# Second attention's projection moved from a block of its own into the first experts' stage

## The reference

```
x = LN(x + softmax attention with RoPE(x))        # layer 0
x = LN(x + sum over 8 experts of w_e * down_e(glu(gate_e x, up_e x)))   # top 2 of 8
x = LN(x + Wo . taylor attention(Wq x, Wk x, Wv x))   # layer 1, 16 heads of 16 features
x = LN(x + capacity-limited experts(x))
```

## Time and profile before

| | us |
|---|---|
| median of 3 runs (850.43 to 851.65) | 851.11 |
| the profiled execution, its own time | 849.08 |
| its span, first to last instruction | 847.0 |
| TensorE busy | 663.2 (78%) |
| VectorE busy | 549.6 (65%) |
| ScalarE busy | 439.5 (52%) |
| GpSimd busy | 406.1 (48%) |

### The profile page before, as it was taken

The page is one execution under the profiler, slowest core; times in us unless marked ns, Lnnn a source line. Parts: engine busy times, 40 slices in busy tenths (PEclk is TensorE's granted clock), DMA queues, the critical chain, the costliest instruction groups (busy, mean ns, idle before and its releaser), DMA issues. The chain is left out here.

```text
span 847.0 us, 18177 instructions
## 1 busy us (share of the span) xinstructions
PE 663.2 (78%) x6567; PEld 417.2 (49%) x6567; DVE 549.6 (65%) x1574; ACT 439.5 (52%) x658; POOL 406.1 (48%) x583
## 2 busy tenths in 40 slices
PE   7748999999869999999977759999996414987500
PEld 3423555555535666666653436767674203555400
DVE  5967888888558898888897653454456883222126
ACT  5433777777745555555526656676763540332102
POOL 7854777777740000000016765666664503788743
PEclk9975999999989999999999988999998755999765
DMA  4773463432000000000004889777851070355354
GB/s 158 240 228 97 122 182 98 119 87 70 4 1 1 1 1 2 1 1 1 2 0 156 253 269 215 190 187 189 198 140 48 11 205 24 79 119 100 32 98 121
DMA packets 134982, 85.79 MB, mean 101 GB/s; under 512 B 11248, under 2 KB 131568, under 8 KB 134768
## 3 DMA queue, kind: packets, MB, share of 16 engines
q1 hardware_dynamic: 128112, 79.33, 34.2%
q0 software_dynamic: 5632, 4.33, 3.7%
q10 hardware_dynamic: 1152, 0.98, 0.4%
HBM read 54.73 MB, written 29.49 MB: 99 GB/s over the span
## 5 line engine op out<-in xcount | busy, mean ns | idle before, releaser
L2143 ACT ACTIVATE a_prob<-a_ps_pair 128x1024 f32<-128x1024 f32 x96 | 93.2, 1024 | 48.1 <-PE a_ps_pair L1979 36.4
L1814 ACT ACTIVATE a_prob<-a_ps_pair 128x1024 f32<-128x1024 f32 x96 | 96.5, 1024 | 13.5 <-PE a_ps_pair L1617 10.7
L2155 POOL TENSOR_SCALAR_AFFINE_SELECT a_prob<-a_prob 128x512 f32<-128x512 f32 (+1 forms) x96 | 76.6, 806 | 51.1 <-ACT a_prob L2143 50.9
L1855 POOL TENSOR_SCALAR_AFFINE_SELECT a_prob<-a_prob 128x512 f32<-128x512 f32 (+1 forms) x96 | 75.6, 789 | 41.2 <-ACT a_prob L1814 40.6
L1753 DVE TENSOR_REDUCE a_mx<-a_ps_pair 128x4 f32<-128x1024 f32 x64 | 77.7, 1220 | 24.3 <-PE a_ps_pair L1658 22.5
L922 POOL TENSOR_SCALAR xn<-xn,stats,norm_b_rstd 128x128 f32<-128x128 f32 x8 | 6.4, 806 | 175.0 <-POOLq L411 175.0
L478 PEld LDWEIGHTS m_ps_n<-wd,m_act 128*128 128x128 f32 x512 | 66.3, 192 | 29.1 <-issue 27.4
L701 ACT ACTIVATE m_up<-m_ps_u,m_bup 128x512 f32<-128x512 f32 x64 | 44.0, 688 | 65.5 <-PE m_ps_u L466 65.5
L590 DVE SCALAR_TENSOR_TENSOR xn<-m_ps_n,m_wt,xn 128x128 f32<-128x128 f32 x256 | 71.7, 342 | 0.2 <-DVE xn L590 0.2
L478 PE MATMUL m_ps_n<-wd,m_act 128*128 128x128 f32 x512 | 67.5, 275 | 1.0 <-DVE xn L590 0.8
L466 PE MATMUL m_ps_u<-m_x1T,wgu 128*128 128x512 f32 x128 | 67.2, 607 | 0.0
(11 more groups left out here) (289 smaller groups left out, 1530.6 us busy)
## 6 DMA issues: line engine op xcount, KB each, us to landing
qst<-scratch_q SPq DMA_DIRECT2D x64, 128.0 KB, 3.0
kst<-scratch_k SPq DMA_DIRECT2D x64, 128.0 KB, 3.1
scratch_q<-p_parts SPq DMA_DIRECT2D x16, 384.0 KB, 2.4
scratch_k<-p_parts SPq DMA_DIRECT2D x16, 384.0 KB, 2.7
qst<-scratch_q SPq DMA_DIRECT2D x32, 192.0 KB, 2.9
kst<-scratch_k SPq DMA_DIRECT2D x32, 192.0 KB, 3.4
c_w<-in_w SPq DMA_DIRECT2D x8, 578.0 KB, 4.0
scratch_q<-parts SPq DMA_DIRECT2D x16, 256.0 KB, 2.5
```

The costliest lines, as they stand in the source:

```text
L1814: nc.scalar.activation(prob[:, r % 6, :], pair[(0, 2, 1)[j]][:, :], ACT.Exp, scale=scale, bias=0.0).then_inc(s_e, 1)
L1855: nc.gpsimd.affine_select(out=blk, in_=blk, compare_op=ALU.is_ge, fill=0.0, base=0, pattern=[[0, n], [1, P]], channel_multiplier=-1).then_ ...
L2143: nc.scalar.activation(prob[:, r % 6, :], pair[r % 2][:, :], ACT.Square, scale=scale, bias=1.0).then_inc(s_e, 1)
L2155: nc.gpsimd.affine_select(out=blk, in_=blk, compare_op=ALU.is_ge, fill=0.0, base=0, pattern=[[0, n], [1, P]], channel_multiplier=-1).then_ ...
```

## The change

The projection of layer 1 becomes steps in `expert_layer0`, and the block `project_layer1` goes. A chunk's rows are normalised as soon as its experts are done: VectorE takes the statistics and a seed of the root, GpSimd refines it in three Newton turns (14 small instructions, each waiting for the one before), ScalarE normalises two tiles and GpSimd two. Five units after that, in six consecutive units, TensorE's turn ends with one step each: the four transposes, four projections, and v. All of these use one PSUM bank, `ps_d`, so each projection waits until the residual of the one before has been taken. VectorE takes a residual first in its turn. The last chunk (`tail`) has no units behind it; it comes after the loop and uses the four banks of gate and up. The bias of all chunks now uses `ps_r`, and its units are moved by one or two. Scratch is laid out by sequence, a store is two DMAs, and four slots are loaded ahead.

```diff
-BUFS1, AHEAD1 = 4, 2
+BUFS1, AHEAD1 = 4, 4
-        turn_at = [E - 1] + [E * c + 2 for c in range(1, NCH)]
-        bias_at = [E + 1] + [E * c + 4 for c in range(1, NCH)]
+        turn_at = [E - 2] + [E * c + 3 for c in range(1, NCH)]
+        bias_at = [E - 1] + [E * c + 5 for c in range(1, NCH)]
+        stats_at = [E * c + E + 1 for c in range(NCH - 1)]
+        next_at = [E * c + E + 5 for c in range(NCH - 1)]
+        next_steps = {n0 + i: (c, i) for c, n0 in enumerate(next_at) for i in range(6)}
 # SyncE
+                    for b in range(2):
+                        sp.dma_start(scratch[i // 2][2 * c + b, :, half:half + P, :].rearrange("s p t -> p s t"),
+                                     parts[:, n % PBUFS, :, T * b:T * b + T]).then_inc(s_store[n % PBUFS], 16)
+                    if 7 <= n < 7 + AHEAD1:
...
+                        load_slot(sp, n - 7, stacks, scratch, s_first)
 # TensorE
+                def turn_next(c):
+                    pe.wait_ge(s_x2a, 2 * c + 2)
+                    pe.wait_ge(s_x2p, 2 * c + 2)
...
+                def project(n):
+                    c, i = n // 4, n % 4
+                    pe.wait_ge(s_xT2, c + 1)
+                    if c < tail:
+                        after(pe, s_r1, n if i else 0)
+                    nc.tensor.matmul(projected(n)[:, :], wqk[:, i, :], x2T[:, c % 2, :], start=True, stop=True).then_inc(s_proj, 1)
...
                 for n in (units - 2, units - 1):
                     reduce(n)
+                for n in range(units, max(next_steps) + 1):
+                    next_layer(*next_steps[n])
+                turn_next(tail)
+                for i in range(4):
+                    project(4 * tail + i)
+                project_v(tail)
 # VectorE
                 for n in range(3, units):
+                    if n - 1 in next_steps and 1 <= next_steps[n - 1][1] < 5:
+                        residual(4 * next_steps[n - 1][0] + next_steps[n - 1][1] - 1)
                     clip(n)
...
+                    if n in stats_at:
+                        row_stats(stats_at.index(n))
+                    if n - 1 in stats_at:
+                        seed_root(stats_at.index(n - 1))
                 for n in (units - 2, units - 1):
                     accumulate(n)
-                row_stats(NCH - 1)
-                merge_rows(NCH - 1)
+                row_stats(tail)
+                seed_root(tail)
+                for n in range(units - 1, max(next_steps) + 1):
+                    if 1 <= next_steps[n][1] < 5:
+                        residual(4 * next_steps[n][0] + next_steps[n][1] - 1)
+                for i in range(4):
+                    residual(4 * tail + i)
 # ScalarE, after take_gate(n)
+                    if n in next_at:
+                        renormalise(next_at.index(n))
+                    if n in next_steps:
+                        next_layer(*next_steps[n])
 # GpSimd
                 for c in range(NCH):
+                    refine_root(c)
                     for i in range(4):
...
+                        lo(4 * c + i)
```

More of the change, by code:

```diff
@@ L369, in expert_layer0 @@
         bns = sb("bns", [P, NTILE, 6])
+        wqk, wv1 = consts["later"]["wqk1"], consts["later"]["wv1"]
+        var2, root, rstd2, shift2 = [sb(n, [P, NTILE]) for n in ("var2", "root", "rstd2", "shift2")]
+        x2T = sb("x2T", [P, 2, CH])
+        resid = sb("resid", [P, 2, CH])
+        parts = sb("parts", [P, PBUFS, NPART, CH], BF16)
         ps_g = [ps(f"ps_g{i}", [P, CH]) for i in range(2)]
@@ L407, in expert_layer0 @@
+        s_lo = sem("lo_done")
+        s_store = [sem(f"parts_stored{i}") for i in range(PBUFS)]
+        s_first = sem("first_stacks_loaded")
+        s_vp = sem("v_projected")
+        s_vc = sem("v_copied")
+        s_ones = sem("ones_set")
         groups = ((0, 2), (2, NCH))
         units = E * NCH
[L409 to L411 removed]
+        turn_at = [E - 2] + [E * c + 3 for c in range(1, NCH)]
@@ L457, in add_bias @@
                         here = slice(t * P, (t + 1) * P)
-                        last = nc.tensor.matmul(ps_bias[c % 2][:, here], wT[:, c % 2, here], bd[:, :], start=True, stop=True)
+                        last = nc.tensor.matmul(ps_r[:, here], wT[:, c % 2, here], bd[:, :], start=True, stop=True)
                     last.then_inc(s_bm, 1)
@@ L739, in _ @@
                         copy_weights(turn_at.index(n))
+                    if n in next_at:
+                        renormalise(next_at.index(n))
+                    if n in next_steps:
+                        next_layer(*next_steps[n])
+                for n in range(units, max(next_steps) + 1):
+                    next_layer(*next_steps[n])
+                renormalise(tail)
+                copy_x2(tail)
+                hi(4 * tail)
+                for n in range(4 * tail + 1, 4 * tail + 4):
+                    hi(n)
+                    mid(n - 1)
+                copy_v(tail)
+                mid(4 * tail + 3)
             @block.gpsimd
@@ L750, in _ @@
                         nc.gpsimd.memset(wT[:, :, :], 0.0).then_inc(s_wTz, 1)
[L752 to L790, removed]
-        x2T = sb("x2T", [P, 2, CH])
-        resid = sb("resid", [P, 4, CH])
-        parts = sb("parts", [P, 8, 3, CH], BF16)
-        ps_qk = [ps(f"ps_qk{i}", [P, CH]) for i in range(4)]
-        ps_x = [ps(f"ps_x{i}", [P, CH]) for i in range(2)]
-        ps_v = ps("ps_v", [P, CH])
-        s_ones = sem("ones_set")
-        s_inv = sem("spread_inverted")
-        s_x2 = sem("tile_normalised")
-        s_x2p = sem("tile_normalised_by_pool")
-        s_xp = sem("x_transposed")
-        s_xT = sem("x_rows_copied")
-        s_proj = sem("qk_projected")
-        s_hi = sem("hi_done")
-        s_r1 = sem("residual_done")
-        s_mid = sem("mid_done")
-        s_lo = sem("lo_done")
-        s_store = [sem(f"parts_stored{i}") for i in range(8)]
-        s_first = sem("first_stacks_loaded")
-        s_vp = sem("v_projected")
-        s_vc = sem("v_copied")
-        def part(c, i, level):
-            return parts[:, 4 * (c % 2) + i, PART_ORDER[i // 2][level], :]
-        with nc.Block() as block:
-            @block.sync
-            def _(sp):
@@ L941, in invert_seed, with load_slot @@
+def load_slot(sp, u, stacks, scratch, done):
+    h0 = UH * (u % 2)
+    for st, sc, runs in zip(stacks, scratch, (SLOT_RUNS["q"], SLOT_RUNS["k"])):
+        src = sc[u // 2, :, :, :].rearrange("s (d h) t -> (s d) h t", h=H)[:, h0:h0 + UH, :]
+        for s0, part, n in runs:
+            sp.dma_start(st[FD * s0:FD * (s0 + n), u % BUFS1, :, :], src[FD * part:FD * (part + n), :, :]).then_inc(done, 16)
 def invert_seed(nc, ve, sem, var, x, t, out):
```

268 lines of the change are left out of this document (139 added, 129 removed).

## The result

The changed kernel takes 855.26 us (median of 5 runs, 853.52 to 855.97) where the kernel before took 850.43 beside it (848.81 to 851.65): ratio 1.0057, 95% interval 1.0041 to 1.0072, 4.8 us slower. The forecast was 852.3, 1.2 us slower.

A forecast was written before the change was run, and what follows sets the result against it. TensorE was taken to fill the expert stage, while no engine fills the projection block. 35.6 us added before unit 63 less 34.4 saved behind it gave 1.2 slower, 852.3 us; own range 850 to 855, 8 in 10 845.5 to 859.5.

The forecast's parts named there:

- Inserted work, 30.0: Before unit 63: TensorE's added transposes, projections and v matmuls, 4.78 us a chunk, paid one for one, together 30.0 us.
- Waits of 0.35 a chunk: Expert units: TensorE waits about 0.2 us for v's bank and 0.15 for renormalised tiles, 2.1 for six chunks.
- Chunk 0, 3.5: Chunk 0's transposes wait for a late root and tiles: 3.9 us, of which 3.5 counted after clearing VectorE's backlog.
- I take 0.28: GpSimd's 14 root steps priced at 0.28 us each, from a 16-element chain, so 3.9 us a refinement.
- TensorE would have come to these transposes at 295.6: Chunk 0: when TensorE would reach the transposes, against tiles ready at 299.5, which gave the 3.9 us wait.
- Cover of 1.7 us in the later chunks: Later chunks: root and tiles done at 14.6 us, TensorE at the transposes at 16.3, leaving 1.7 spare.
- Tail 40.2: From unit 63's start to the next stage: a serial chain at 1.2 GHz, 40.2 us, 34.4 less than before.
- rival 1: Tail runs at the fast clock level: about 4 to 5 us less, 848; chance 0.28.
- The stage behind, nothing: Next stage: two more slots loaded ahead and rows lying together were taken to save nothing.
- rival 4: Loads did hold back the next stage's start and the new layout frees it: 4 us less, 848; chance 0.04.
- Rival 2: GpSimd and VectorE exclude each other, making GpSimd late to every chunk: 5 to 9 us more, 859; chance 0.22.
- Rival 3: TensorE's clock falls in chunk 0's wait of some 2.5 us: slow spells cost 3 us, 855; chance 0.06.

The follow-up runs named there:

- the last kernel: Chunk 0's early seed with reordered, filled tail, plus from chunk 1 on statistics one unit later and root on VectorE, and tail residual earlier: 837.62 us, ratio 0.9859.
- The early seed in chunk 0: Against the changed kernel, only chunk 0's root seed runs in the unit of its row statistics, not one unit later: 851.38 us, ratio 1.0020.

## Why the prediction was right or wrong

Slower was the likeliest side, and the kernel is slower; most of the mechanism held, while one path was half wrong and several terms were mis-sized. 855.26 lies just past the forecast's own range (850 to 855) and inside the range for 8 times in 10. The forecast of 1.2 us was the difference of two sums of about 35, smaller than the miss of a single term below, so its side owes something to luck. By the prediction's own terms:

- *Inserted work, 30.0.* Right: units 3.47 apart, and the doubled projections and the last kernel's chunk of 26.97 show it one for one.
- *Waits of 0.35 a chunk.* 27.45 - 22.21 - 4.78 = 0.46, 0.7 us more over six chunks. It is all v's wait, 0.48 and not 0.2; the transposes' 0.15 isn't seen in the steady chunk.
- *Chunk 0, 3.5.* This is the step that failed by most. From unit 13 to 21 it is 33.33 us, 5.88 over a steady chunk; before, the same stretch was 22.71, 0.50 over. So 5.4, 1.9 more than forecast. The seed came when it was forecast, 48.6 us after the stage's first instruction (293.9 - 245.26 there, 296.31 - 247.67 here). What failed is "I take 0.28": the 14 steps took 5.56, 0.40 each, beside VectorE, and the two tiles 1.82 for 1.7; together 1.8 more, which is the miss. A second step failed without showing in the sum: "TensorE would have come to these transposes at 295.6", 50.3 us after the stage's first instruction. It came 54.2 us after it (303.86 - 1.97 = 301.89), because it had waited 2.24 for VectorE and then ran at the low clock. With steps of 0.28 the tiles would have been ready at about that moment (303.76 - 1.8), so that 3.5 would have come out nearly right whatever the root did. The early seed in chunk 0 shows the two apart: 2.0 of the 5.4 hung on the root, and the rest on VectorE's backlog, which no run here takes away.
- *Cover of 1.7 us in the later chunks.* The refinement took 1.3 us longer there and left GpSimd's side about 0.6 (its tiles done at 358.15, transposes at 358.78). Chunk 4 went over, by 1.28: there the seed came 1.3 us late as well, behind a product of VectorE that had been held up by a low part (last section). Together these terms make unit 63 later by 39.4 where 35.6 was forecast.
- *Tail 40.2.* Measured 39.7, its steps at the low level as taken; rival 1 (the fast level) did not happen. The last chunk's projections and low parts took 10.0 us for 11.1, as the clock rose during them, and the other terms together 0.6 more than forecast.
- *The stage behind, nothing.* 0.5 us shorter in one trace, and two slots rather than four made no difference: rival 4 is refuted for the loads. The layout of the rows alone was not tried.

So the net is 1.2 + 3.8 - 0.5 = 4.5, where the trace shows 4.6 up to the next stage. Rival 2 had its mechanism right: the engines do exclude each other, and chunks 0 and 4, where that shows, make 3.2 of the 3.8 us by which unit 63 came later than forecast. But in the other chunks the cover held the 5.2 us of root, so its 5 to 9 us did not come; the changed kernel's longest root, 5.56, is just under the 5.6 at which it was to decide. Rival 3's fall of the clock did come in chunk 0 (3.41 us at 0.50), between two waits, and the tiles, not the clock, set the end there; with the early seed both are gone, so the runs don't separate them.

## What to carry to other kernels

When work moves from an idle block under a full engine, the full engine pays it one for one, so the gain must come from the serial end that is left: here the move alone lost 4.8 us, and shortening that end (39.6 to 28.3 us) brought the kernel under the one before. Price a chain of small GpSimd steps with VectorE at work beside it (here 0.40, not 0.28), and hold its cover against the busiest chunk. Starting the chain a unit sooner there gains only as much as the next wait in line allows: of 3.24 us, 2.0 were left, since VectorE was late too. A late arrival of 2 us on TensorE can cost nearly twice that, since the clock falls behind it.

## What the runs showed of the hardware

A GpSimd step of 4 elements takes 0.20 us alone and 0.70 to 0.72 where a product of VectorE has started just before it. The other way round, in chunk 4, VectorE's and GpSimd's timelines:

```profile
404.19 1.66 DVE L675 SCALAR_TENSOR_TENSOR m_act<-m_glu,m_upc 128x512 f32<-128x512 f32 x1 [0.45 <-issue]
```

```profile
404.14 1.16 POOL L939 TENSOR_TENSOR m_parts<-m_resid,m_parts 128x512 bf16<-128x512 f32 x1 [2.71 <-ACT m_parts L829]
```

The product, 0.69 alone, lasts 1.66 where the low part starts 0.05 us before it: it ends 0.55 us after the low part's end (405.30), as if held until then. The kernel before left this open for two operands from SBUF. The Trainium skill, in SBUF — State Buffer (section "Who interferes with whom"), says that an instruction of VectorE with two SBUF inputs contends with one of GpSimd that reads SBUF; these rows agree, also for a GpSimd step with one tensor operand (298.95, 0.70). The tensor_scalar of the earlier trace rows, which the prediction counted as agreeing, has one tensor input, so that row does not bear on this sentence.

The traces put chunk 4's loss down to this product. The chunk's seed is ready 2.85 us after its unit's start (407.37 - 404.52), in a steady chunk 1.54 (351.16 - 349.62), and the transposes then wait:

```profile
414.93 0.63 PE L540 MATMUL m_ps_d<-ident,xn 128*128 128x128 f32 x4 [1.09 <-issue]
```

The traces with two slots ahead and with TensorE's waits filled have such a product (1.66 us) in chunk 4 as well, and the same wait (1.08). With chunk 0's early seed no product of the stage takes over 0.8 us, and the wait is gone. No run forces or forbids the meeting.

TensorE's clock fell to half behind waits of 2.0 to 2.3 us, though not behind each: of two waits of 2.34 one was followed by matmuls at 1.75 to 1.91, the next by 1.10. Behind waits of 0.88 us, and of 1.75 in chunk 0 with the early seed, it did not fall.
